# Layer norm applied by ScalarE, the output bias folded in by GpSimd ahead of the product, and the first layer's down projection interleaved with the first attention maxima

## What is computed

```
def layer(x):
    n = layernorm(x)                       # (x - mean) / sqrt(var + 1e-5)
    a = attention(n) @ w_o + b_o           # the "output bias" b_o; layer 2: a row scale, no bias
    s = branch(n)                          # layer 0: low-rank SwiGLU whose down projection ends in silu
                                           # layer 1: four streams mixed by a 50-step Sinkhorn, silu
                                           # layers 2 and 3: routed low-rank experts, silu
    return x + a * s
```

## Time and profile before

| | |
|---|---|
| time, median of 3 runs | 1273.21 us (1271.34 to 1274.51) |
| time of the profiled execution | 1270.83 us |
| its span (first to last instruction) | 1268.8 us |
| PE busy | 1050.2 us, 83% |
| DVE busy | 834.3 us, 66% |
| ACT busy | 565.0 us, 45% |
| POOL busy | 328.4 us, 26% |
| PE clock granted, mean | 0.908 of full |

### The profile page before, as it was taken

One profiled execution on the slowest core, in us unless ns is written; L12 is line 12 of the kernel. 1 busy time (PEld: TensorE's weight loads), 2 busy tenths in 40 slices (PEclk: granted clock), 3 DMA queues, 4 the chain that ended last, 5 costly groups with the idle time before them and its releaser, 6 DMA issues.

```text
span 1268.8 us, 19873 instructions
## 1 busy us (share of the span) xinstructions
PE 1050.2 (83%) x7480; PEld 444.8 (35%) x7480; DVE 834.3 (66%) x1475; ACT 565.0 (45%) x797; POOL 328.4 (26%) x516
## 2 busy tenths in 40 slices
PE   2889999897898997865535639899899988999998
PEld 2434444343333444531211302223233234434344
DVE  6322222001786884798997999888978787876874
ACT  2533333100565664502123335858645767354671
POOL 2145444001776311000002136360000042011230
PEclk9989999998698998786657758999999999999999
DMA  8421220001321011020000032140012111220200
GB/s 306 143 73 55 72 75 25 1 1 49 89 64 35 26 37 60 14 63 22 16 0 1 27 102 74 48 148 28 20 35 69 51 44 39 64 76 26 69 17 34
DMA packets 54899, 69.72 MB, mean 55 GB/s; under 512 B 9526, under 2 KB 43444, under 8 KB 54800
## 3 DMA queue, kind: packets, MB, share of 16 engines
q1 hardware_dynamic: 50828, 58.57, 14.7%
q0 software_dynamic: 3984, 9.98, 2.8%
HBM read 49.45 MB, written 18.82 MB: 54 GB/s over the span
## 4 chain that ended last, share of the span: by engine, by line
DVE 30%; PE 30%; issue 4%; ACT 4%; POOL 3%; DMA 3%; SPq 1%; ACTq 0%; DVEq 0%; POOLq 0%
DVE w_mx L1320 14%; PE w_banks L667 8%; PE w_po L1250 7%; PE w_banks L1230 4%; PE w_banks L1202 3%; DVE w_region L1933 2%; ACT w_pr L1270 2%; PE w_banks L1190 2%; PE w_banks L1584 2%; DVE w_region L1893 1%; DVE w_region L1930 1%; DVE w_region L1928 1%; DVE w_region L1926 1%; DMA w_ks<-stack_scratch 1%; DVE w_region L1924 1%
## 5 line engine op out<-in xcount | busy, mean ns | idle before, releaser
L1320 DVE TENSOR_REDUCE w_mx<-w_banks 128x2 f32<-128x1024 f32 (+3 forms) x352 | 368.6, 1086 | 94.0 <-PE w_banks L1202 92.6
L1270 ACT ACTIVATE w_pr<-w_banks 128x1024 f32<-128x1024 f32 (+1 forms) x312 | 304.2, 1014 | 214.3 <-PE w_banks L1230 201.9
L1308 POOL TENSOR_SCALAR_AFFINE_SELECT w_pr<-w_pr 128x512 f32<-128x512 f32 (+1 forms) x184 | 107.8, 591 | 396.1 <-ACT w_pr L1270 396.1
L1230 PE MATMUL w_banks<-w_qs,w_ks 49*128 49x512 f16 (+7 forms) x832 | 125.4, 346 | 42.9 <-DVE w_mx L1320 30.3
L1202 PE MATMUL w_banks<-w_ks,w_qs 48*128 48x512 f16 (+7 forms) x832 | 139.4, 351 | 25.1 <-DVE w_mx L1320 11.3
L1250 PE MATMUL w_po<-w_pr,w_vz 128*17 128x512 f32 (+7 forms) x1152 | 142.8, 533 | 17.1 <-DVE w_vz L909 6.7
L78 PE MATMUL f_pp<-xt,sl_region 128*128 128x512 f16 x672 | 149.2, 383 | 2.4 <-POOL sl_region L504 2.4
L480 DVE TENSOR_TENSOR sl_region<-sl_region,f_pp 128x512 f32<-128x512 f32 x28 | 19.3, 688 | 120.3 <-ACT sl_region L495 120.3
L78 PEld LDWEIGHTS f_pp<-xt,sl_region 128*128 128x128 f16 x672 | 65.2, 99 | 83.8 <-issue 5.6
L1230 PEld LDWEIGHTS w_banks<-w_qs,w_ks 49*128 49x128 f16 (+1 forms) x832 | 36.0, 97 | 147.1 <-issue 58.3
L1190 PE MATMUL w_banks<-mask_half,ident_half 64*128 64x128 bf16 (+1 forms) x768 | 64.7, 248 | 17.9 <-DMA w_ks<-stack_scratch 8.6
(11 more groups left out here) (221 smaller groups left out, 1478.9 us busy)
## 6 DMA issues: line engine op xcount, KB each, us to landing
stack_scratch<-sl_region SPq DMA_DIRECT2D x102, 128.0 KB
w_qs<-stack_scratch SPq DMA_DIRECT2D x96, 96.0 KB, 2.3
sl_region<-in_L_gu SPq DMA_DIRECT2D x14, 512.0 KB
w_stage<-in_L_w POOLq DMA_DIRECT2D x36, 128.0 KB, 2.4
sl_region<-in_L_down SPq DMA_DIRECT2D x14, 256.0 KB
stack_scratch<-p_qk SPq DMA_DIRECT2D x24, 128.0 KB
w_ks<-stack_scratch SPq DMA_DIRECT2D x32, 96.0 KB, 2.5
bw_stage<-in_L_w SPq DMA_DIRECT2D x4, 640.0 KB, 10.1
```

Of the source, the lines that this page charges most:

```text
L1230: mm = pe.matmul(g.banks.pair_at(f)[:, half, at:at + T - q0], g.ks[base:base + self.rows + 1, k_slot, k_place, j * P:(j + 1) * P], g.qs[ba ...
L1270: act.activation(g.probs.at(self.pr_fill[s])[:, :, 0:width], g.banks.pair_at(self.s_fill[s])[:, :, 0:width], ACT.Exp, scale=self.a.scale). ...
L1308: pool.affine_select(out=diagonal, in_=diagonal, compare_op=ALU.is_ge, fill=0.0, base=0, pattern=pattern, channel_multiplier=-1).then_inc( ...
L1320: dve.tensor_reduce(out, g.banks.pair_at(self.m_fill[m])[:, :, 0:heads * keys].rearrange("q h (p k) -> q h p k", k=keys), AX.X, ALU.max).t ...
```

## The change

1. `d0` is taken out of `swiglu_low_rank`. The down projection becomes a stage of ticks, `Down` (letter `d`, four matmuls each), in a block `down_and_maxima` of its own, before the barrier. It is interleaved, after the list `FIRST_TURNS`, with 4 ticks `q`, the first 18 ticks `m` and 3 ticks `t` of a00. The buffers for them are allocated earlier. This block has no share for POOL.
2. `TURNS` is written anew. It begins with `w32`.
3. `Normalise`: DVE makes -mean x rstd (one small instruction), and ACT applies scale and shift to the 4 tiles.
4. `Outward`: POOL adds `branch * row` to the residual before the product is ready (two instructions for each tile; in layer 2 one, which multiplies the branch by the row). DVE then multiplies the product by the branch straight from the bank and adds it. The bank is held until that multiplication, where it was held until the addition of the row. A tick of the product may come only when the whole branch has been emitted (`needs`).

```diff
+class Down(Stage):
+    def pe(self, pe, t):
+        i, k = divmod(t, self.parts)
+        if i == NT:
+            return
+        if k == 0:
+            self.g.banks.free(pe, self.fills[i])
+        mm = partial(pe, self.g.banks.at(self.fills[i]), lambda part, c: self.gated[:, part, c, i * P:(i + 1) * P],
+                     lambda part, c: self.w[:, part, c, :], range(self.chunks), PRODUCTS, 4 * k, 4 * k + 4)
+        if k == self.parts - 1:
+            mm.then_inc(self.made.sem, 1)
...
 class Normalise(Stage):
+        if t in (6, 7):
+            act.wait_ge(self.shift.sem, self.shift.at + 1)
+            for i in (2 * t - 12, 2 * t - 11):
+                act.activation(self.xn[:, i, :], self.g.x_res[:, self.b * NI + i, :], ACT.Identity,
+                               bias=self.g.sd[:, 0, i:i + 1], scale=self.g.sd[:, 2, i:i + 1]).then_inc(self.normed.sem, 1)
...
-            for i in (2 * t - 12, 2 * t - 11):
-                dve.tensor_scalar(self.xn[:, i, :], x[:, i, :], g.mv[:, i, 0:1], g.sd[:, 2, i:i + 1],
-                                  ALU.subtract, ALU.mult).then_inc(self.normed.sem, 1)
+            dve.scalar_tensor_tensor(g.sd[:, 0, :], g.mv[:, :, 0], -1.0, g.sd[:, 2, :], ALU.mult, ALU.mult
+                                     ).then_inc(self.shift.sem, 1)
...
 class Outward(Stage):
-            dve.tensor_tensor(self.att[:, i, :], g.banks.at(self.fills[i]), self.row,
-                              ALU.mult if self.a.binary else ALU.add).then_inc(self.out.sem, 1)
+            dve.wait_ge(self.based.sem, self.based.at + i + 1)
+            dve.tensor_tensor(self.att[:, i, :], g.banks.at(self.fills[i]), self.sl[:, i, :], ALU.mult
+                              ).then_inc(self.gated.sem, 1)
...
+    def pool(self, pool, t):
+        if t == self.mul_at[0]:
+            self.take_bias(pool, 0)
+            self.take_bias(pool, 1)
+        i = self.tile_at(self.turn_at, t - 1)
+        if i is not None and i > 1:
+            self.take_bias(pool, i)
+
+    def take_bias(self, pool, i):
...
+        sl, x = self.sl[:, i, :], g.x_res[:, self.b * NI + i, :]
+        if self.a.binary:
+            pool.tensor_tensor(sl, sl, self.row, ALU.mult).then_inc(self.based.sem, 1)
+            return
+        pool.wait_ge(self.turned.sem, self.turned.at + i + 1)
+        pool.tensor_tensor(self.att[:, i, :], sl, self.row, ALU.mult).then_inc(self.biased.sem, 1)
+        pool.wait_ge(self.biased.sem, self.biased.at + i + 1)
+        pool.tensor_tensor(x, x, self.att[:, i, :], ALU.add).then_inc(self.based.sem, 1)
...
+FIRST_TURNS = "q4 d6 " + "m1 d5 " * 6 + "t1 " + "m1 d5 " * 6 + "t1 d2 " + "m1 d3 " * 6 + "t1 d3"
+
 TURNS = """
-    w10 m5 q m2 q2 l m t m q m3 e m e t m e m e m2 v e m v e q e v t w2 q e o m2 v m e m v m e2 o m w v e2 w v m w e
...
+    w32 q e5 q v e q e v2 e o m2 v e m v e m2 o e v m e2 v m t e m e v m3 v2 m2 o e v e t e m2 v o2 e2 m v e m v q e
...
+def down_and_maxima(nc, top, g, stack_dram, gated, w):
+    merge({"d": [all_of(down)], "q": [some_of(first.stacks, 0, SLOTS + 1)], "m": [some_of(first.maxima, 0, SLOTS * first.n_m)],
+           "t": [some_of(first.turns, 0, SLOTS)]}, FIRST_TURNS, order, g.emitted, g.banks)
```

More of the change, by code:

```diff
@@ new lines, in weave @@
+    n11 = Normalise(g, 1, (o01.added, NI), sl[:, 1])
+    p11 = Project(g, h[1], 1, lambda part, c, cols: w1[:, part, c, cols], col1, v_row1, vz(1, 1), n11, stacks[1], [])
+    a11 = Attend(g, h[1], 1, vz(1, 1), att(1), stacks[1], p11, a10)
+    s1 = Streams(g, 1, sl[:, 1], w24, wb, base24[:, :], gate[:, :], n11, [])
+    s1.begins_after = [(n11, n11.ticks[-1])]
+    balance = Balance(g, (s0, s1))
+    o10 = Outward(g, h[1], 0, lambda part, c: wo1[:, part, c, :], o_rows[:, 1, :], att(0), sl[:, 0], done(a10),
+                  s0, [], n10)
@@ new lines, in weave @@
+    n20 = Normalise(g, 0, (o10.added, NI), att(0))
+    p20 = Project(g, h[2], 0, lambda part, c, cols: sign_qkv[:, c, cols], g.binary.cols, g.binary.rows[:, 0:h[2].n_v],
+                  vz(2, 0), n20, stacks[2], [])
+    a20 = Attend(g, h[2], 0, vz(2, 0), att(0), stacks[2], p20, a11)
+    split2 = Split(g, split_rows("L2_w_ra", w_ra) + [(ins["L2_w_b"], w_b[:, 0, :], w_b[:, 1, :])])
+    o11 = Outward(g, h[1], 1, lambda part, c: wo1[:, part, c, :], o_rows[:, 1, :], att(1), sl[:, 1], done(a11),
+                  s1, [], n11)
@@ new lines, in weave @@
+    n21 = Normalise(g, 1, (o11.added, NI), att(1))
+    p21 = Project(g, h[2], 1, lambda part, c, cols: sign_qkv[:, c, cols], g.binary.cols, g.binary.rows[:, 0:h[2].n_v],
+                  vz(2, 1), n21, stacks[2], [])
+    a21 = Attend(g, h[2], 1, vz(2, 1), att(1), stacks[2], p21, a20)
+    r20 = Routed(g, 0, w_ra, w_b, 1, sl[:, 0], n20, [split2.done(), small.done()], [(o10.gated, NI)])
+    split3 = Split(g, split_rows("L3_w", w3) + split_rows("L3_wo", wo),
+                   [(p11.made, len(p11.chunks)), (p11.v_made, p11.v_units), s1.ready(), (o01.made, NI)])
@@ new lines, in weave @@
+    rows3 = Loads(g, "third", [(g.cos, ins["cos"]), (g.sin, ins["sin"]),
+                               (o_rows[:, 0, :], ins["L3_o_bias"].partition_broadcast(P))],
+                  [(o11.made, NI), s1.ready(), (p11.v_out, p11.v_units), (o01.based, NI)])
+    o20 = Outward(g, h[2], 0, lambda part, c: sign_o[:, c, :], g.binary.rows[:, h[2].n_v:], att(0), sl[:, 0], done(a20),
+                  r20, [], n20)
+    n30 = Normalise(g, 0, (o20.added, NI), att(0))
+    rope_free = [(p21.made, len(p21.chunks)), (p21.v_made, p21.v_units)]
```

368 lines of the change are left out of this document (183 added, 185 removed).

## The result

The changed kernel takes 1317.88 us (median of 4 runs, 1316.27 to 1321.06) against 1272.28 us of the kernel before in the same comparison. The ratio is 1.036, with a 95% interval of 1.033 to 1.039: slower by 45.6 us. I had predicted 1297 us, with a range of 1274 to 1316. The direction is right, 21 us are missing.

The account below looks back on a forecast made before the run. Three engines take turns after the barrier, then PE leads, DVE bounds the Sinkhorn steps, and both bound the end. 1270.8 + 37 - 3 + 0 + 0 - 10 = 1294.8, with 2.4 added 1297 us; range 1274 to 1316.

Parts of the forecast that it names:

- behind them: Last Sinkhorn step to 743.8 us: 0 (-5 to +9), DVE's other work filling its waits for POOL's bias.
- The block, +12: Down projection before the barrier: 18 units of maxima beside PE's matmuls make it 12 us longer (8 to 14).
- Weights ahead of the masks, +40: Behind the barrier: 32 pieces on POOL instead of ten, 63.4 us, make the first mask 40.0 us later.
- What comes back before o00: First mask to o00's first transpose: 61 us instead of 76.3, so 15 us back (10 to 25).
- The balance at o00: Start of o00: 12 + 40 - 15 = 37 us late.
- The 6 us for the clock: Behind the first mask: PE at half clock for some 20 us costs up to 10 us, taken as 6.
- o00 to the Sinkhorn steps, -3: o00 to first Sinkhorn step: DVE spared 10.2 us, against leftover maxima and scores; -3 us (-10 to +5).
- The Sinkhorn steps, 0: Sinkhorn steps: a chain on DVE, 50 steps with the same number of maxima among them, no change.
- 743.8 us to the end, -10: Last stage: DVE spared 20.8 us, half counted, -10 us (0 to -21); ACT's norms and POOL's bias hidden.
- DVE gives it all back: Rival: from o00 on, DVE's 36 us saved pay the 37 us late; 1274 or 1264 us, chance 0.13.
- The slow clock stays: Rival: PE stays longer at half clock in the first groups or falls at mask waits; 1307 to 1312 us, chance 0.09.
- POOL is starved by DVE: Rival: POOL's biases of o10 and o11 get nothing beside DVE's two-operand work; 1306 to 1315 us, chance 0.10.

Follow-up runs that it names:

- e5: Kernel before, order kept, with only the down projection woven with the first 18 maxima; norm and bias on DVE: 1282.76 us, ratio 1.008.
- e1: Changed kernel with ten pieces of weights ahead of the first mask and 22 strewn among the scores before o00: 1283.45 us, ratio 1.007 to the kernel before.
- e4: Kernel before with its first 32 pieces of weights all ahead of everything behind the barrier: 1309.8 us, ratio 1.029.
- e12: Kernel before with 17 of the first 29 pieces of weights split by POOL during the down projection: 1268.86 us, ratio 0.996.
- e13: Kernel before with 17 early pieces of weights and the first 18 maxima in the down projection, norm and bias on DVE: 1261.98 us, ratio 0.992.
- e3: Changed kernel with the output bias back on DVE, in the new order: 1316.82 us, ratio 1.033 to the kernel before.
- e14: Changed kernel with strewn pieces, 17 of them split by POOL during the down projection: 1270.09 us, ratio 0.997 to the kernel before.
- e17: Changed kernel with strewn pieces (e1) and ACT's norm applied to one column of each tile: 1280.92 us.
- e18: Changed kernel with strewn pieces (e1) and POOL's bias taken for one column of each tile: 1272.33 us, ratio 1.000 to the kernel before.
- e8: Kernel before with ACT applying the norm; order, bias and down projection as before: 1297.88 us, ratio 1.020.
- e15: Kernel before with the output bias left out, DVE's 32 row instructions given to no engine: 1263.3 us, ratio 0.992.
- e16: Kernel before with DVE's norm applied to one column of each tile: 1268.04 us, ratio 0.9975.

## Why the prediction was off

The 21.5 us between 1294.8 us and the profiled execution (1316.27 us) are, by the table above, -2.0 + 1.5 up to o00, 5.8 from there to the Sinkhorn steps, 7.2 in the steps, 1.7 behind them and 7.3 in the last stage.

*The block, +12.* Measured +10.0, and e5 shows 10.5 us at the end. Right.

*Weights ahead of the masks, +40.* The mask came 38.7 us later. Right, and e1 and e4 show by undoing and by adding it that it costs 34 and 36 us.

*"What comes back before o00", -15.* The balance at o00 came out right (+36.5 for my +37), partly by luck: 12.2 us came back, and the block and the mask were some 3 us better than I had them. The cause had the wrong size too. That POOL has no pieces left is worth 4 us (e4: 41 late, 36.7 at o00). The rest was the new order: with the pieces strewn it reached o00 in 90.9 us where e5 in the old one needed 98.5. I had read the eight groups' rate from a stretch that has pieces in it and credited all of the difference to them. The 6 us for the clock were too many: from PE's first product with the values the granted clock was 0.50 (1.2 GHz) for 3.7 us, from 381.7 to 385.4 us, where I had reckoned with some 20. From there to o00 it was full, and PE was busy nearly all the time:

```profile
385.40:444.90 59.50, 55.61 (x694) 23.11 (x686) 48.20 (x60) 40.79 (x50) 19.78 (x37) 1.00 0.21 48
```

So the groups took longer than the rate of the earlier trace rows gave, and less was lost to the clock: from the mask to o00 it is 64.0 us for my 61.

*o00 to the Sinkhorn steps, -3.* Measured +2.8. PE leads this stage and got 3.0 us more to do in it (117.98 us against 115.01), while DVE got only 0.6 less (95.49 against 96.06). I had set DVE's relief against it. With the new order and the norm on ACT this stage took 133 to 135 us in every kernel, and 130 to 132 us with the old order and norm and bias on DVE (before, e4, e5, e12, e13).

*The Sinkhorn steps, 0.* Measured +7.2. This is a step that failed: "A chain on DVE, 50 steps with the same number of maxima among them: 0." The number is the same, 16, but the chain stands still for maxima whose products PE makes late, 8.7 us against 1.7. The 7 us belong to the new order, not to the parts. The steps took 134 to 136 us in every kernel with that order (e1 to e3, e14, e17, e18) and 127 to 128 us in every one with the old (e4, e5, e8 to e13, e15, e16), whichever engine had norm or bias. Against e5, e1 is 7.6 us ahead at o00, loses 10.5 us of it by the last step, and gets 2.5 us behind it: about zero in all. The new order with strewn pieces and with norm and bias both on DVE was not run, so the order's own price is not separated from theirs.

*743.8 us to the end, -10.* Measured -2.7. This is the other step that failed: "ACT has the norms instead, at 57% busy, and POOL the bias at 23%: hidden." The gross value of DVE's savings was well sized. I had 13 us in all (3 and 10), and e15 and e16 give 8.5 + 3.7 = 12.2. But I had set the receivers at nothing, and in the order made for them POOL costs 10 to 11 us (e18) and ACT at most 2.5 (e17). 12.2 gained against 10 to 13.5 spent agrees, within what such differences can tell, with the 0.7 us between e5 and e1. Of POOL's price, 5.9 us lie between the last step and the next layer's first maximum, where I had taken 0 as well and DVE's relief hid most of it (+1.7). The rest lies in the last stage: 517.5 us in e18, 520.6 to 524.6 in the kernels with the same order and POOL's full bias (the change, e1, e14). POOL's share of busy time said nothing: the bias can begin only when the branch is ready, and then it is a chain of two instructions a tile.

*The rivals.* "DVE gives it all back" is wrong by the sum above. "The slow clock stays" is wrong: it stayed for 3.7 us in front of o00, as said above. From 579 to 713 us the granted clock was 0.68, but before it was 0.65. "POOL is starved by DVE" named the right engine and, for o10, the right place, but the wrong one of the two was held up on the chain. POOL's first bias there lost 1.6 us (2.83 for 1.26), while DVE's four instructions beside the others lost 3.8. The other part of the price is what POOL's own instructions take at the end of the program (1.26 us undisturbed, 1.59 beside DVE's addition), a place that the rival does not name. The Trainium skill, "GPSIMD Engine Reference", section 4.1, gives two-input elementwise work on GpSimd as about twice VectorE's time; 1.26 against 0.69 us here, and the trace agrees. The rule was in my text and I used it only to ask if POOL was free.

By the runs the sum is: 1272.3 + 10.5 (e5) + 0.7 (e1 against e5) + 34.4 (the change against e1) = 1317.9 us. It closes by the way it is made, from kernel to kernel; what it tells is that nearly all of the loss is the block and the weights in front of the masks, and that the rest of the change together is worth nothing.

## What to carry to other kernels

Work that is moved from a busy engine to an idle one is priced on the receiver too, at its own duration, at the place where its input becomes ready; a low busy share hides nothing there. It can also slow the instructions of the engine that it was taken from, as at o10. In an order written out by hand a moved step brings its misfit: 26 and 33 us here for parts whose relief of DVE is worth 4 and 9, so an edit and its order are tested together, and one without the other says nothing about the edit. And where three engines take turns, relieving one shows nothing until the next is relieved as well: two edits of +10 and -3 us gave -10 together.

## What the hardware showed that I had not expected

Instructions of POOL and DVE that read two operands from SBUF hold each other up, and either engine can be the one that loses. At o10, in the rows above, POOL's first bias took 2.83 us instead of 1.26 while DVE's eight ran at their usual 0.34 us each. Then DVE's four took 1.02, 1.42, 1.35 and 1.42 us, and beside each of the last three one of POOL's ran, of 1.26 to 1.31 us. At the end of the changed kernel, in the timeline of DVE and of POOL:

```profile
1298.27 0.95 DVE L1045 TENSOR_TENSOR x_res<-x_res,att 128x512 f32<-128x512 f32 x1
...
1306.97 0.69 DVE L1045 TENSOR_TENSOR x_res<-x_res,att 128x512 f32<-128x512 f32 x1
```

```profile
1297.40 1.27 POOL L1070 TENSOR_TENSOR att<-sl_region,w_o_rows 128x512 f32<-128x512 f32 x1
1298.74 1.59 POOL L1072 TENSOR_TENSOR x_res<-x_res,att 128x512 f32<-128x512 f32 x1
```

DVE's addition begins 0.40 us before POOL's L1070 ends and takes 0.95 us instead of 0.69. POOL's L1072 begins 0.48 us before that addition ends and takes 1.59 instead of 1.26. So a short overlap costs each some two thirds of it. One column instead of 512 still costs 0.265 us on DVE, 0.37 on ACT and 0.19 on POOL (medians of e16, e17 and e18).
